# A macaron block: gelu of two layers written into its own PSUM bank, and 12 of 16 later norms turned by a transposing DMA

## What is computed

```python
def ffn(x):                                   # 128 -> 512 -> 512 -> 512 -> 128, ternary weights
    h = silu(x @ w1.T * s1) * (x @ w2.T * s2)
    h = gelu(h @ h1.T * sh1)                  # layer 2
    h = gelu(h @ h2.T * sh2)                  # layer 3
    return h @ w3.T * s3

def att(x):
    h = layernorm(x) * gamma + beta
    keys, values = h @ Wk.T + bk, h @ Wv.T + bv
    w = exp((keys @ Wka.T + bka) / sqrt(128))
    w = w / cumsum(w, axis=1)                 # over the 256 rows of a sequence
    return cumsum(w * keys, axis=1) * values

x = x + 0.5 * ffn(layernorm(x))
x = x + att(layernorm(x))
x = x + 0.5 * ffn(layernorm(x))
```

## Time and profile before

| | |
|---|---|
| median of 3 runs | 367.62 us (367.56 to 367.99) |
| profiled execution, first to last instruction (span) | 366.2 us |
| its own time beside the span | not recorded; the median lies 1.4 us above the span |
| PE, DVE, ACT, POOL busy | 359.0, 319.5, 283.6, 171.9 us |
| granted clock of PE | 0.999 of full speed |

### The profile page before, as it was taken

How to read it: one execution, slowest core, us unless ns; L and a number is a source line. 1 busy time by engine, 2 the same in 40 slices (tenths; PEclk the granted TensorE clock), 3 DMA queues, 4 the chain that set the end, 5 groups by cost and what they waited for, 6 DMA issues and landing times.

```text
span 366.2 us, 5192 instructions
## 1 busy us (share of the span) xinstructions
PE 359.0 (98%) x1572; PEld 284.6 (78%) x1572; DVE 319.5 (87%) x542; ACT 283.6 (77%) x463; POOL 171.9 (47%) x259
## 2 busy tenths in 40 slices
PE   7999999999999999999999999999999999999995
PEld 2678888778877887887878787887878877888885
DVE  5999788989989989999999989999999799947742
ACT  5898777886897789777876969868888796777763
POOL 3583375694124578512794545663574740520000
PEclk9999999999999999999999999999999999999999
DMA  7725504042000302100221021022024010050001
GB/s 255 242 96 167 166 2 115 0 113 62 1 2 0 99 18 58 59 4 0 56 63 57 3 58 59 0 59 58 0 60 117 1 57 2 0 143 2 30 1 59
DMA packets 17534, 21.44 MB, mean 59 GB/s; under 512 B 7392, under 2 KB 8672, under 8 KB 17248
## 3 DMA queue, kind: packets, MB, share of 16 engines
q1 hardware_dynamic: 16640, 20.15, 19.9%
q10 hardware_dynamic: 864, 0.93, 0.8%
HBM read 18.89 MB, written 2.19 MB: 58 GB/s over the span
## 4 chain that ended last, share of the span: by engine, by line
PE 97%; DVE 1%; ACT 0%; issue 0%; POOL 0%; POOLq 0%; DVEq 0%
PE hid_ps L654 62%; PE gate_ps L654 8%; PE y_ps L654 8%; PE up_ps L654 7%; PE y_ps L673 2%; PE xt_ps L847 2%; PE xt_ps L843 2%; PE xt_ps L850 2%; PE y_ps L763 1%; PE up_ps L718 1%; PE gate_ps L718 1%; DVE full L1092 0%; PE xt_ps L654 0%; DVE gate L1080 0%; DVE xt_sb L1152 0%
## 5 line engine op out<-in xcount | busy, mean ns | idle before, releaser
L654 PE MATMUL hid_ps<-act_hi,hi_h 128*128 128x512 f32 (+1 forms) x368 | 146.5, 398 | 0.0
L654 PE MATMUL hid_ps<-act_lo,hi_h 128*128 128x512 f32 (+1 forms) x368 | 143.1, 389 | 0.0
L1102 DVE TENSOR_TENSOR act_lo<-full,act_hi 128x512 fp32r<-128x512 f32 x157 | 117.3, 769 | 20.9 <-ACT act_hi L918 17.7
L911 ACT ACTIVATE full<-hid_ps,vec 128x512 f32<-128x512 f32 x123 | 84.3, 686 | 53.3 <-PE hid_ps L654 36.9
L654 PEld LDWEIGHTS hid_ps<-act_lo,hi_h 128*128 128x128 f32 x368 | 69.2, 188 | 16.3 <-issue 1.4
L654 PEld LDWEIGHTS hid_ps<-act_hi,hi_h 128*128 128x128 f32 x368 | 69.2, 188 | 16.0 <-issue 1.4
L918 ACT ACTIVATE act_hi<-full 128x512 fp32r<-128x512 f32 x127 | 78.6, 628 | 1.6
L580 POOL TENSOR_TENSOR xnt<-xt_sb,wide 128x512 f32<-128x512 f32 x22 | 31.6, 1437 | 49.5 <-DMA wide<-rows 43.8
L654 PE MATMUL hid_ps<-act_hi_second,hi_h 128*128 128x512 f32 x128 | 52.1, 407 | 0.0
L654 PE MATMUL hid_ps<-act_lo_second,hi_h 128*128 128x512 f32 x128 | 50.0, 390 | 0.0
L894 ACT ACTIVATE tanh<-gate_ps,s_half 128x512 f32<-128x512 f32 x60 | 40.6, 682 | 8.9 <-PE gate_ps L654 8.8
(11 more groups left out here) (168 smaller groups left out, 542.7 us busy)
## 6 DMA issues: line engine op xcount, KB each, us to landing
wide<-rows SPq DMA_DIRECT2D x44, 256.0 KB, 3.7
out<-xt_sb SPq DMA_DIRECT2D x7, 256.0 KB, 3.1
raw_h<-h2t SPq DMA_DIRECT2D x4, 256.0 KB, 7.0
x_sb<-x SPq DMA_DIRECT2D x1, 1024.0 KB, 5.0
xt_sb<-xt SPq DMA_DIRECT2D x1, 1024.0 KB, 5.0
x_sb<-x SPq DMA_DIRECT2D x3, 256.0 KB, 5.5
raw_h<-h1t SPq DMA_DIRECT2D x2, 256.0 KB, 6.0
xt_sb<-xt SPq DMA_DIRECT2D x2, 256.0 KB, 4.1
```

The costliest lines, as they stand in the source:

```text
L654: mm = eng.matmul(ps, w, a, start=(first and n == 0), stop=(last and n == len(seq_) - 1))
L911: eng.activation(full23[m % 2][:, :], home23(n, T, m)[:, :], ACT.Gelu, scale=col("sh1" if n == 2 else "sh2", m)).then_inc(s_gelu[n], 1)
L1102: eng.tensor_tensor(act_lo[a][:, m, :], full[m % 2][:, :], act_hi[a][:, m, :].bitcast(F32), ALU.subtract).then_inc(s_lo[n], 1)
```

## The change

Three things.

1. **Gelu in place.** For tiles 1 to 15, gelu of layers 2 and 3 writes its result back into the bank that it reads (`gelu_out`). The high part and the low part then read the bank, and PE's next group there waits for the low part (`s_lo`) where it waited for the gelu. The waits of gelu for the SBUF tiles fall away.
2. **Rows by DMA.** For a1 to a7 and tiles 8 to 12 (`BY_DMA`), PE's turn is replaced by three steps: POOL splits the `xt_sb` tile into planes of its low and high 16-bit halves (`split`), SP issues one transposing DMA over 128 x 1024 values of 16 bits (`turn`), ACT puts the halves together again (`join`), and DVE takes the statistics from that SBUF tile. The buffers are parts of `x_sb` whose rows are used up. a0 and tiles 13 to 15 are still turned on PE.
3. **Orders anew.** START and STEPS are rewritten for all engines.

The core of the diff:

```diff
+BY_DMA = (("att", 1), ("att", 2), ("att", 3), ("att", 4), ("att", 5), ("att", 6), ("att", 7), ("ffn", 8), ("ffn", 9), ("ffn", 10), ("ffn", 11), ("ffn", 12))
...
+        def planes_out(k):
+            return planes_b[k % 2][:, :].rearrange("c (h j p) -> c h j p", h=2, j=SUB)
+
+        def planes_in(t):
+            return xt_tile(t).bitcast(U16).rearrange("c (p j h) -> c h j p", j=SUB, h=2)
...
+        def gelu_out(n, T, m):
+            return home23(n, T, m) if T > 0 else full23[m % 2]
...
+            def turn(kind, t):
+                k = dma_of[kind, t]
+                eng.wait_ge(s_split, k + 1)
+                if k >= 2:
+                    eng.wait_ge(s_joined, k - 1)
+                eng.dma_start_transpose(turned_b[k % 2][:, :].rearrange("p (b f) -> p b f", f=P),
+                                        planes_b[k % 2][:, :]).then_inc(s_turned[k % 2], 16)
...
+            def split(kind, t):
+                k = dma_of[kind, t]
+                eng.wait_ge(*((s_x1, t + 1) if kind == "att" else (s_x2, t - NT + 1)))
+                if k >= 2:
+                    eng.wait_ge(s_turned[k % 2], 16 * (k // 2))
+                eng.tensor_copy(planes_out(k), planes_in(t)).then_inc(s_split, 1)
...
                 elif n == 2 and m < 2:
-                    eng.wait_ge(s_gelu[3], MC * T - MC + m + 3)
+                    eng.wait_ge((s_lo if T > 1 else s_gelu)[3], MC * T - MC + m + 3)
                 elif (n, T) == (3, 0) and m < 2:
                     eng.wait_ge(*((s_full1, MC + 2), (s_gate, MC + 1))[m])
                 elif n == 3 and m < 2:
-                    eng.wait_ge(s_gelu[2], MC * T + m + 3)
+                    eng.wait_ge(s_lo[2], MC * T + m + 3)
                 else:
-                    eng.wait_ge(s_gelu[n], MC * T + m - 1)
+                    eng.wait_ge((s_lo if T > 0 else s_gelu)[n], MC * T + m - 1)
...
-                if n == 2 and m < 2:
-                    if T > 0:
-                        eng.wait_ge(s_lo[3], MC * T - MC + m + 3)
-                elif n == 3 and m < 2:
-                    eng.wait_ge(s_lo[2], MC * T + m + 3)
-                else:
-                    eng.wait_ge(s_lo[n], MC * T + m - 1)
-                eng.activation(full23[m % 2][:, :], home23(n, T, m)[:, :], ACT.Gelu,
+                if T == 0 and m >= 2:
+                    eng.wait_ge(s_lo[n], m - 1)
+                elif (n, T) == (3, 0):
+                    eng.wait_ge(s_lo[2], m + 3)
+                eng.activation(gelu_out(n, T, m)[:, :], home23(n, T, m)[:, :], ACT.Gelu,
                                scale=col("sh1" if n == 2 else "sh2", m)).then_inc(s_gelu[n], 1)
...
+            def join(kind, t):
+                k = dma_of[kind, t]
+                eng.wait_ge(s_turned[k % 2], 16 * (k // 2 + 1))
+                eng.wait_ge(s_bn, SUB * norm_of[by_dma[k - 2] if k >= 2 else ("ffn", 4 + k)] + SUB)
+                eng.activation(halves_out(k), halves_in(k), ACT.Copy).then_inc(s_joined, 1)
```

Of the orders, the places that the prediction speaks of. ACT's start, old and new:

```diff
-        "hi:w1 bits:w2 hi:w2 z vec:s1 0:t bits:h1.1 bits:h1.3 0:tanh.0 0:tanh.1 0:tanh.2 0:high1.0 0:high1.1",
...
+        "bits:w2 hi:w1 hi:w2 vec:s1 z 0:t bits:h1.1 0:tanh.0 0:tanh.1 bits:h1.3 0:tanh.2 0:high1.0 0:high1.1 "
```

PE in the new order, around tiles 6 to 8 (items without a prefix are tile 6 for p2 and p3, tile 7 for p1), and its end:

```diff
+        "5:p3.2 5:p3.3 a2:values p2.0 p2.1 p1.2 p1.3 p2.2 p2.3 p4 p3.0 p3.1 8:p1.0 p3.2 p3.3 8:p1.1 a3:logits "
+        "7:p2.0 7:p2.1 8:p1.2 a3:keys 8:p1.3 7:p2.2 7:p2.3 9:p1.0 6:p4 7:p3.0 7:p3.1 a3:values 7:p3.2 7:p3.3 "
...
+        "15:p1.2 14:p2.2 14:p2.3 15:p1.3 13:p4 14:p3.0 14:p3.1 14:p3.2 14:p3.3 p2.0 p2.1 p2.2 p2.3 p4 p3.0 "
+        "p3.1 p3.2 last:p4a last:p3.0 last:p3.1 last:p4b last:p4c.0 last:p4c.1",
```

PE in the old order, tile 6 and the end:

```diff
-        "a2:values p1.1 p2.0 p2.1 p2.2 p1.2 p2.3 p1.3 p4 p3.0 p3.1 p3.2 p3.3",
...
-        "p2.0 p2.1 p2.2 p2.3 p1.0 p1.1 p4 p1.2 p3.0 p3.1 p1.3 p3.2 p3.3",
-        "p2.0 p2.1 p2.2 p2.3 p4 p3.0 p3.1 p3.2 last:p4a last:p3.0 last:p3.1 last:p4b last:p4c.0 last:p4c.1",
```

Split and join of a1 and a2 in the queues of POOL and ACT (items without a prefix: tile 4 in the first line of POOL, 2 or 3 in ACT's first, tile 3 or 4 in its second):

```diff
+        "2:xn.0 2:xn.1 3:xn.0 hi:w3 3:xn.1 a0:norm norm a0:xn.0 a0:xn.1 a1:split xn.0 xn.1 a1:norm 5:norm "
+        "6:norm a0:weight a1:xn.0 a1:xn.1 5:xn.0 5:xn.1 a2:split a0:dt a2:norm 7:norm 6:xn.0 6:xn.1 a2:xn.0 "
...
+        "a0:t gelu2.2 high2.2 high1.1 gelu2.3 high2.3 4:t a1:join gelu3.0 tanh.3 high3.0",
...
+        "high2.3 5:t tanh.3 gelu3.0 high1.2 high3.0 a2:join gelu3.1 a1:t high3.1 5:tanh.0 gelu3.2 high3.2 "
```

More of the change, by code:

```diff
@@ L52 @@
     "SP": (
[L53 to L68, removed]
+        "park wide 3:park 3:wide a0:park 4:park a0:wide 4:wide a1:turn a1:park 5:park a1:wide 5:wide a2:turn "
+        "6:park a2:park 6:wide a2:wide 7:park",
+        "",
+        "a3:turn 7:wide 8:turn 9:turn a4:turn",
+        "a3:park 8:park a3:wide 8:wide",
+        "9:park",
+        "",
+        "9:wide 10:turn a5:turn a4:park a4:wide 10:park",
+        "10:wide a5:park a5:wide",
+        "11:turn",
+        "",
+        "11:park",
+        "",
+        "11:wide 12:turn a6:turn 12:park 12:wide a6:park a6:wide a7:turn 8:store 13:park a7:park 13:wide "
+        "a7:wide park wide 15:park 15:wide",
+        "",
+        "",
+        "9:store 10:store 11:store 12:store 13:store store",
     ),
     "POOL": (
[L71 to L84, removed]
-        "",
[19 rows of a table added]
         "",
@@ L190 @@
 BY_PE = (0, 1)
+BY_DMA = (("att", 1), ("att", 2), ("att", 3), ("att", 4), ("att", 5), ("att", 6), ("att", 7), ("ffn", 8), ("ffn", 9), ("ffn", 10), ("ffn", 11), ("ffn", 12))
 AGGREGATE = 2
 LINES = 4
-AHEAD = {"stats": 2, "aggr": 2, "veps": 2, "norm": 2, "z": 2, "t": 1, "p1": 1, "tanh": 1, "gate": 1,
+AHEAD = {"split": 2, "turn": 2, "join": 2, "stats": 2, "aggr": 2, "veps": 2, "norm": 2, "z": 2, "t": 1, "p1": 1, "tanh": 1, "gate": 1,
          "up": 1, "high1": 1, "low1": 1, "u": 2, "park": 2, "wide": 2, "xn": 2, "p4": -1, "dt": -1, "store": -1}
@@ L234, in macaron_block @@
         xnt_b = [sb(f"xnt_{i}", [P, TOK]) for i in range(2)]
+        spare = [x_sb[:, i * TOK:(i + 1) * TOK] for i in range(6)]
+        planes_b = [spare[i].bitcast(U16) for i in (0, 1)]
+        turned_b = [spare[i].bitcast(U16) for i in (2, 3)]
+        rows_b = [spare[i] for i in (4, 5)]
         rows = nc.dram_tensor("rows", [LINES, 2 * TOK], F32).ap()
@@ L318, in macaron_block @@
         s_agg, s_centred, s_xn = sem("s_agg"), sem("s_centred"), sem("s_xn")
+        s_split, s_joined = sem("s_split"), sem("s_joined")
+        s_turned = [sem(f"s_turned_{i}") for i in range(2)]
         s_parked = [sem(f"s_parked_{i}") for i in range(LINES)]
@@ L399, in macaron_block @@
         att_norms = {n for (kind, _), n in norm_of.items() if kind == "att"}
-        turned = [sum(1 for k, m in norm_of.items() if m <= n and (k[0] == "att" or k[1] >= NT))
+        by_dma = sorted((key for key in norm_of if key in BY_DMA), key=norm_of.get)
+        dma_of = {key: k for k, key in enumerate(by_dma)}
+        turned = [sum(1 for k, m in norm_of.items() if m <= n and k not in BY_DMA and (k[0] == "att" or k[1] >= NT))
                   for n in range(len(norm_of))]
@@ L626, in emit @@
                     (xn_add, xn_mult)[chunk]("ffn" if stage == "xn" else "att", t)
+                elif stage in ("split", "att_split"):
+                    split("ffn" if stage == "split" else "att", t)
                 elif stage == "att_weight":
@@ L950, in emit @@
                     or_bits(t, chunk or 0)
+                elif stage in ("join", "att_join"):
+                    join("ffn" if stage == "join" else "att", t)
                 elif stage == "vec":
@@ L1099, in low @@
                     eng.wait_ge(s_lo[1], m)
[L1100 removed]
+                full = full1[m % 2] if n == 1 else gelu_out(n, T, m)
                 a = first_act(T) if n == 1 else n
[L1102 removed]
+                eng.tensor_tensor(act_lo[a][:, m, :], full[:, :], act_hi[a][:, m, :].bitcast(F32),
                                   ALU.subtract).then_inc(s_lo[n], 1)
```

26 lines of the change are left out of this document (17 added, 9 removed), and 221 rows, old and new, of tables (SECOND_LAYER, START, STEPS).

## The result

The changed kernel is slower: 375.61 us median of 4 runs (373.5 to 377.1) against 367.81 for the kernel before on the same chip, ratio 1.0199, 95% interval 1.0161 to 1.0238. I had forecast 364.8 and a range up to 370.0.

What follows compares the result with a forecast made beforehand. PE (TensorE) was taken to bound the kernel, with DVE nearly full beside it. 366.2 - 5.6 - 0.4 + 2.2 + 1.0 = 363.4, plus 1.4 around the span: 364.8 us, range 361.6 to 370.0.

Steps and rivals of the forecast that it cites:

- the +1.0 of the middle: Attention stretch, 38 short bank reuses: lows late behind DVE reciprocals cost 1.0 us, bounds 0 and 5.6.
- Twelve turns, -5.6: 12 of 16 row turns leave PE at 0.47 us each: 5.6 us gained, called the one sure term.
- Joins, splits, transfers, 0: Twelve norms: POOL splits 1.3 us, DMA landings 4.5, ACT joins 1.0, all covered by idle time, costing nothing.
- rival C: Transposing DMAs land late, 7.0 us, and stall ACT at the joins: about 379 us; chance 0.14.
- the estimate of 10.5 us: Landing time of a transposing DMA if its eight blocks went one after the other.
- no gain from it: Attention stretch: lows reading a bank could save DVE 6 us, but DVE stays about as full, so counted as nothing.
- The end, +2.2: Bank stalls at 4:p3.2 and in tiles 14 and 15, waiting for lows: 2.2 us, bounds 0 and 2.4.
- The start, -0.4: ACT's read of h1.3 bits moves behind two tanhs: 0.4 us gained, bounds 0 and 0.63.
- B: Attention stretch: the bank is the new bound, lows late because DVE is 95% full: 367 to 370; chance 0.24 with D.
- D: The turns on PE were covered by something else, so removing them gains nothing: 369.8 us; chance 0.24 with B.

Runs made afterwards that it cites:

- recips_cut: Changed kernel with the reciprocals of tiles 1 to 7 taken over 16 of 256 columns each (work left out): 371.75 us, ratio 1.0118.
- lows_first: Changed kernel with tiles 14 and 15's gelu in SBUF, plus four DVE lows put earlier, one ACT join later, four stores held back: 370.67 us, ratio 1.0079.
- gelu_to_sbuf: Changed kernel with gelu written to the two SBUF tiles again, with the old waits; DMA rows and new orders stay: 394.22 us, ratio 1.0741.

## Why the prediction was wrong

By the table PE's last product comes 9.1 us later than forecast: 4.6 us are the middle, 3.3 the end, 1.0 the start and 0.5 the stretch up to 100 us (rounded, and 0.3 too much in all). The step that failed most is the +1.0 of the middle: what PE waits there for low parts.

**Twelve turns, -5.6.** They left PE as worked out: 64 transposes became 16. But the term was called sure because the chain showed no gap, and a chain without a gap does not say how far DVE and ACT are behind PE. Run alone, the removal gave 3.0 us. My caveat, that it is worth 5.6 only where PE can go on at once, was right and had no number in the sum. In the new orders the removal was not measured by itself, and what it uncovers is among the lost times of the table.

**The middle, +1.0, is the term that failed: 5.6 was measured.** The mechanism was named (lows that come late to a bank that is now held through the low), and 5.6 was the upper bound; the value was taken near the low end because most reciprocals stood in long distances. Those distances are measured in PE's work. What sits between a bank's last product and its low is ACT's and DVE's order: scans, weights, lows of layer 1, an `xn_lo`, a join. Counting reciprocals alone missed most of it: cutting them gave back 2.1 of the middle, cutting the joins 2.1, with 1.4 in common.

**Joins, splits, transfers, 0.** The copies were within bounds, and the transfers under them: 2.7 us to landing. So rival C falls as priced. With it falls the estimate of 10.5 us, which took the 1309 ns for one block from the Trainium skill's "VectorE: DVE Perf Modes", section "The three transpose paths", eight times one after the other. The Trainium skill's other statement, "Advanced Engine Details and Errata", section "X-Bar Transpose (TRN2)", that such transfers are as fast as regular ones, fits the 2.7 beside 3.8 for a broadcast. What failed is "nothing", because POOL and ACT had idle time. Idle time covers a step only if what it holds back is not wanted at that moment. With gelu in SBUF a split costs DVE about 1.9 us (18.5 us for ten); in the changed kernel the splits cost 1.0 at most, the joins 2.5 (by the ratios) to 3.2 (by the medians).

**Gelu in place, a loss only.** I priced the waits that it makes and noted that lows reading a bank would save DVE 6 us, "no gain from it". The saving was there, 183 of 200 us busy, a low 0.675 us (DVE's busy time in lows, in the window of the earlier trace rows):

```profile
80.00:280.00 200.00, 72.18 (x107) 1.00 0.24 57
```

In these orders it is worth 19 us: without it 394 us. That it can't live in the old orders was right (462).

**The end, +2.2: measured 5.5.** The five bank stalls came at just the places named, 0.46 us at four of them behind 340 us and 0.46 at 4:p3.2, each of the four followed by 0.15 at the next group, 2.4 us in all behind 340. So the stalls that I had counted were priced about right. The other 3 us were not in the sum: 1.8 for tile 15's input with 0.5 behind it, and small ones. I had gone through every wait that the in-place gelu adds, and not through the chain that leads to the last tile's norm in the new order.

**The start, -0.4: +0.6.** It stays open which of the moved bits, statistics and copies made it.

**The rivals.** B came nearest: waits for `act_lo` head PE's list. But its ground, DVE full, is not what the windows show: DVE had 17 us idle in 200. Whether it lacks time or only does the wrong thing first isn't settled: 20 us less of work (recips_cut) gave back 2.1 us, four places put in another order (lows_first) 0.4, since the next thing was then late. D was part of the truth in the old orders (2.6 of 5.6 us). B and D stop at 370, short of 375.6, and C's 379 lies past it for a reason that is not there: each rival had one cause, and the time has several.

## What to carry to other kernels

A bank or buffer that is released later by one engine must be followed through the other engines' orders, not through the distance on the engine that fills it: list what stands ahead of the releasing instruction, with durations. A step that fits into an engine's idle time is free only if it doesn't slow a neighbour; a long POOL operation beside DVE's operations of two SBUF operands cost the DVE its whole length. In a kernel with orders written out by hand, measure a part in the orders that it came with: gelu in place, the DMA rows and the new orders, each by itself, ran 18 to 94 us slower than the kernel before.

## What was new about the hardware

- DVE's subtractions of two SBUF operands took 2.4 us instead of 0.65 while POOL copied (4.88 us for two beside 4.85 of splits); with one operand in a bank, 0.68 beside a split too.
- After PE had waited 1.68 us for a low, gelu_to_sbuf's trace shows products 0.427 apart in place of 0.227 for 3.4 us, and a granted clock of 0.51, the 1.2 GHz level, then 1.00 again (length, busy us of the engines, PEclk):

```profile
221.94 0.64 PE L724 MATMUL hid_ps<-act_lo,hi_h 128*128 128x512 f32 x1 [1.68 <-DVE act_lo L1182]
```

```profile
222.40:225.60 3.20, 3.20 (x9) 2.52 (x8) 3.20 (x7) 1.84 (x3) 2.48 (x7) 0.51 0.01 3
225.60:229.00 3.40, 3.40 (x14) 2.45 (x14) 2.14 (x4) 1.73 (x3) 0.00 (x0) 1.00 0.18 20
```

So this stall was paid nearly twice, 1.6 us more by these rows. Not every one is: in the changed kernel PE lost 1.82 us at tile 15's first products, at 325 us, and the granted clock stayed at 1.00.
- A transposing DMA of 128 x 1024 values of 16 bits landed in 2.7 us (median of 12), faster than the broadcast of as many bytes, 3.8.
- The split, 1024 16-bit values a partition, took 2.07 us on POOL and 2.05 on ACT; the join, as many values, 1.19 on ACT.
